# The third chunk of a graph is seeded by one ScalarE copy over both PSUM banks instead of one copy per bank

## What is computed

```python
def _L0_gnn_ref(x, adj, W1, b1, W2, b2):
    mask = (adj > 0.0).astype(x.dtype)
    xj_proj = x @ W1a
    diff = x[:, :, None, :] - x[:, None, :, :]
    h = jax.nn.relu(xj_proj[:, :, None, :] + diff @ W1b + b1)
    hm = jnp.einsum('bjkh,bjk->bjh', h, mask)
    deg = jnp.sum(mask, axis=-1)
    return hm @ W2 + deg[..., None] * b2
# layer 0
h = jnp.maximum(_layernorm(x, axis=-1), 0.0)
x = x + _L0_gnn_ref(h, adj, W1, b1, W2, b2)
# layer 1
h = jnp.maximum(_layernorm(x, axis=-1), 0.0)
x = x + einsum('bnm,bmf,of->bno', adj, h, W)
```

## Time and profile before

| | |
|---|---|
| median of 3 runs | 849.71 us (849.04 to 850.85) |
| profiled execution | 851.92 us, its span 849.9 us |
| busy: TensorE / VectorE / ScalarE / GpSimd | 95% / 96% / 93% / 72% |
| mean granted TensorE clock | 0.983 of 2.4 GHz |
| seeds L561 | 1024, 506 ns on the mean |
| gathers L400 of the regular chunks | 4096 |
| consumes L804 | 1024 |

### The profile page before, as it was taken

How to read it: one execution, slowest core, us unless ns; L and a number is a source line. 1 busy time by engine, 2 the same in 40 slices (tenths; PEclk the granted TensorE clock), 3 DMA queues, 4 the chain that set the end, 5 groups by cost and what they waited for, 6 DMA issues and landing times.

```text
span 849.9 us, 26682 instructions
## 1 busy us (share of the span) xinstructions
PE 809.7 (95%) x8242; PEld 712.0 (84%) x8243; DVE 820.1 (96%) x2908; ACT 794.5 (93%) x2241; POOL 610.8 (72%) x1164
## 2 busy tenths in 40 slices
PE   3779999999999999999999999999999999999996
PEld 1447888988898889888988898888888988998884
DVE  6989999999999999999999999999999999999994
ACT  4768999999999999999999999999999999999993
POOL 0855777777787777777777777777777777777773
PEclk9779999999999999999999999999999999999998
DMA  9800000000000000000000000000000000000000
GB/s 336 324 1 2 2 14 20 21 15 20 21 20 9 21 21 18 17 21 21 20 9 21 20 21 15 21 20 20 8 20 21 20 14 21 21 20 9 27 1 23
DMA packets 26704, 27.54 MB, mean 32 GB/s; under 512 B 3520, under 2 KB 24512, under 8 KB 25536
## 3 DMA queue, kind: packets, MB, share of 16 engines
q1 hardware_dynamic: 25488, 25.37, 8.8%
q10 hardware_dynamic: 1072, 0.43, 0.2%
HBM read 21.59 MB, written 4.19 MB: 30 GB/s over the span
## 4 chain that ended last, share of the span: by engine, by line
PE 84%; DVE 6%; issue 3%; ACT 3%; POOL 2%; DMA 1%; SPq 0%; ACTq 0%; POOLq 0%; DVEq 0%
PE ring L400 45%; PE ring L428 8%; PE prep L457 4%; DVE acc L804 4%; PE post L494 3%; PE post L500 3%; PE post L487 3%; PE post L488 3%; PE prep L465 3%; PE prep L468 2%; PE prep L463 2%; PE post L492 2%; POOL rstd L969 1%; DMA x_all<-x_nbf_dram 1%; PE prep L459 1%
## 5 line engine op out<-in xcount | busy, mean ns | idle before, releaser
L804 DVE SCALAR_TENSOR_TENSOR acc<-ring,acc 128x384 f32<-128x384 f32 x896 | 491.7, 549 | 0.6
L561 ACT COPY ring<-P 128x384 f32<-128x384 f32 x1024 | 467.5, 506 | 23.4 <-DVE acc L804 10.4
L400 PE MATMUL ring<-PQ,onehot_space 128*128 128x192 f16 x4096 | 418.7, 247 | 5.5 <-ACT ring L561 2.4
L400 PEld LDWEIGHTS ring<-PQ,onehot_space 128*128 128x128 f16 x4096 | 328.7, 99 | 42.7 <-issue 13.5
L900 POOL TENSOR_SCALAR start<-P,spare 128x192 f32<-128x192 f32 x128 | 131.9, 1030 | 135.5 <-ACT P L611 135.0
L924 POOL TENSOR_TENSOR row_space<-row_space 128x192 f32<-128x192 f32 x256 | 153.3, 599 | 29.7 <-ACT row_space L599 14.0
L790 DVE TENSOR_SCALAR onehot_space<-mask_all 128x512 f16<-128x512 f16 x512 | 161.8, 318 | 0.0
L428 PE MATMUL ring<-PQ,owner 128*128 128x384 f16 (+1 forms) x512 | 94.0, 306 | 0.0
L400 PE MATMUL ring<-PQ,onehot_row 128*128 128x192 f16 x768 | 84.4, 246 | 2.0 <-DVE onehot_row L852 2.0
L599 ACT ACTIVATE row_space<-ring 128x576 f32<-128x576 f32 x128 | 83.1, 649 | 0.7 <-PE ring L400 0.7
L804 DVE SCALAR_TENSOR_TENSOR acc<-ring,start 128x384 f32<-128x384 f32 x128 | 71.2, 556 | 6.8 <-PE ring L400 2.5
(11 more groups left out here) (138 smaller groups left out, 1422.0 us busy)
## 6 DMA issues: line engine op xcount, KB each, us to landing
onehot_space<-adj_kbj_dram SPq DMA_DIRECT2D x8, 1024.0 KB, 17.6
adj_again<-adj_kbj_dram SPq DMA_DIRECT2D x128, 64.0 KB, 2.0
x_all<-x_nbf_dram SPq DMA_DIRECT2D x8, 512.0 KB, 18.4
out_dram<-x_all SPq DMA_DIRECT2D x32, 128.0 KB, 1.9
consts<-consts_dram SPq DMA_DIRECT2D x1, 192.0 KB, 2.5
scratch<-w1a_dram ACTq DMA_DIRECT2D x2, 48.0 KB, 4.4
scratch<-w1b_dram ACTq DMA_DIRECT2D x2, 48.0 KB, 6.9
scratch<-b_dram ACTq DMA_DIRECT2D x1, 96.0 KB, 10.2
```

What stands on the lines that cost most here:

```text
L400: last = nc.tensor.matmul(to, hot(s), parts[:, part, H:2 * H], start=False, stop=(part == 1), skip_group_check=True)
L561: return nc.scalar.copy(slots[to][:, bank_], src.unsqueeze(1).broadcast_to([N, PER_BANK, H]))
L804: return nc.vector.scalar_tensor_tensor(sums, slots[to][:, bank_], 0.0, start[:, :, :] if first else sums, ALU.max, ALU.subtract if first ...
```

## The change

The third chunk of each graph (i = 2, listed in WHOLE) gets one copy of 768 elements over both banks, `seed_both`, in place of two copies of 384. It raises `seeded` once, so a graph now raises it seven times instead of eight; SEEDS holds the running count ahead of each chunk. TensorE waits, for both banks of that chunk, for the count that the one copy raises. The other chunks keep a copy and a count per bank. What the copies write is unchanged.

```diff
+SEEDS = (0, 2, 4, 5, 7)
+WHOLE = (2,)
...
                             for bank_ in range(BANKS):
-                                pe.wait_ge(seeded, (b * REGULAR + i) * BANKS + bank_ + 1)
+                                pe.wait_ge(seeded, b * SEEDS[-1] + (SEEDS[i + 1] if i in WHOLE else SEEDS[i] + bank_ + 1))
                                 dst = [(s, slot(place(u, i), s)) for s in range(PER_BANK * bank_, PER_BANK * (bank_ + 1))]
                                 gather(dst, parts, hot).then_inc(gathered, 1)
...
+            def seed_both(to, src):
+
+                return nc.scalar.copy(slots[to], src.unsqueeze(1).unsqueeze(1).broadcast_to([N, BANKS, PER_BANK, H]))
+
...
-                        for bank_, consumed in enumerate((half_summed, summed)):
-                            if i in (0, 1) and exists(b - 1):
-                                act.wait_ge(consumed, b * REGULAR - 1 + i)
+                        if i in WHOLE:
                             if i == 3:
-                                act.wait_ge(consumed, b * REGULAR + 1)
-                            seed(place(u, i), P[:, u % 2, :], bank_).then_inc(seeded, 1)
+                                act.wait_ge(summed, b * REGULAR + 1)
+                            seed_both(place(u, i), P[:, u % 2, :]).then_inc(seeded, 1)
+                        else:
+                            for bank_, consumed in enumerate((half_summed, summed)):
+                                if i in (0, 1) and exists(b - 1):
+                                    act.wait_ge(consumed, b * REGULAR - 1 + i)
+                                if i == 3:
+                                    act.wait_ge(consumed, b * REGULAR + 1)
+                                seed(place(u, i), P[:, u % 2, :], bank_).then_inc(seeded, 1)
```

## The result

The changed kernel takes 858.54 us against 850.83 for the kernel before, medians of 17 runs each taken side by side: ratio 1.0092, interval 1.0072 to 1.0112, 7.7 us slower. Forecast were 5.7 us more, in a range of 848 to 866.

The account below looks back on a forecast made before the run. The prediction took a slackless ring through TensorE, VectorE and ScalarE, once per pair of graphs, as the bound. 63 pairs x 0.09 us = 5.7 us on the median 849.71 gave 855.4 us, range 848 to 866.

Parts of the forecast that it names:

- the bounds: Limits on the whole copy's length around the forecast 0.82 us: 0.79 us below, 0.92 us above.
- S-to-L478: Even graph, third chunk's first seed start to TensorE's L478: about 2.15 us before, 2.19 to 2.29 forecast.
- 63 x 0.09: 63 graph pairs, each longer by the even graph's middle delay of 0.09 us: 5.7 us slower.
- the ring: Even-graph seeds, TensorE, VectorE and back, 11.95 us a pair; delay added to S-to-L478 lengthens the pair fully.
- second ring: Runs over odd-graph seeds and the even graph's first consume; delayed 0 to 0.09 us, beside the first, not added.
- where the 0.10 us goes: ScalarE's saving per graph brings P and later work earlier, ends waiting for VectorE's consume, and shortens nothing on the ring.
- Rival A: L790 slips behind GpSimd's row sums L924 in even graphs, up to 0.33 us each; 862 to 876 us; chance 0.12.
- Rival B: Odd-graph L790 moves further behind L924 and loses 0.18 us; 846.4 or 850.5 us; chance 0.18.
- Rival C: ScalarE bounds the kernel, so 0.10 us less a graph gives 12.8 us less, 836.9 us; chance 0.05.
- Rival D: The even-graph delay falls into idle time, so no effect, 849.7 us; chance 0.07.

Follow-up runs that it names:

- e1_wait: Kernel before with two copies kept, but the third chunk's gathers for both banks wait for the second copy; 858.91 against 851.38 us.
- e7_whole3: Changed kernel with the whole copy given to the fourth chunk instead of the third; 878.06 us against 850.41 for the kernel before.
- e2_filler: Changed kernel plus a one-column ScalarE copy behind the fourth chunk's seeds, filling the saved 0.1 us; 854.44 us against 851.38 for the kernel before.
- f2_light_whole: Changed kernel with GpSimd's row sums and second fp16 part of P cut to one column each; 859.11 us against 850.41 for the kernel before.
- f3_light_whole_hold: f2_light_whole with GpSimd's start sums held back to a later VectorE consume; 846.16 us against 852.27 for the kernel before.
- the three kernels with the hold: Start sums held back on the kernel before, the changed kernel and e5_order_whole; 896.39, 895.41 and 894.98 us against 852.27.
- e3_short: Kernel before with ScalarE's PQ copy cut from 384 to 272 columns, so P comes earlier; 846.72 against 851.38 us.
- f1_light: Kernel before with GpSimd's row sums and second fp16 part of P cut to one column each; 841.69 against 850.41 us.
- e4_order: Kernel before with ScalarE's code_row and ownerT copies moved behind the fourth chunk's seeds; 850.62 against 851.38 us.
- e5_order_whole: Changed kernel with code_row and ownerT moved behind the fourth chunk's seeds; 849.05 us against 850.41 for the kernel before.
- g1_hold: Kernel before with only GpSimd's start sums held back to a later VectorE consume, nothing left out; 896.39 against 852.27 us.

## Why the prediction was right, and where it was not

**The copy.** Forecast 0.82 us and a spacing of 0.72 to 0.73; measured 827 ns and 0.73. The interpolation from a copy's own slope was right and the bounds weren't needed. The Trainium skill (ScalarE: Activation LUTs, What ACT_TABLE_LOAD costs) gives 186 ns + 0.833 ns an element, an estimate of 0.83 us for this copy; the 827 ns agree.

**S-to-L478.** Forecast 2.19 to 2.29, measured 2.21 in the graph shown and 2.27 on the mean of all even graphs, 0.09 more than before, the forecast's middle; 2.38 in e1_wait and 2.37 in e7_whole3 in the graphs shown (2.37 and 2.44 on the mean), each as their expectations had it. This step holds.

**From the delay to the time.** Forecast 63 x 0.09 = 5.7 us (2.5 to 8.8). With that delay of 0.09 and P unmoved, e2_filler costs 3.0 us; e1_wait, with one of 0.20 (2.374 against 2.176 on the mean), costs 7.5. That is 33 and 38 us for each microsecond of delay in the even graph, not 63. What is wrong is "the ring has no slack": it was read from one pair, in which VectorE waits 0.10 us for the odd graph's first gathers. Over the whole trace before, VectorE waits ahead of 66 of 128 first consumes (43 of 64 in odd graphs, 23 in even ones), so a delay passes on only in part, and L790, which gets shorter with the delay, gives some of it back. In f2_light_whole, f3_light_whole_hold and the three kernels with the hold nearly all of VectorE's idle time ahead of first consumes stands in even graphs (15.5 of 16.9 us in f3_light_whole_hold): that is the prediction's second ring, over the odd graph's seeds, which it did not add.

**The step that failed** is "where the 0.10 us goes ... it shortens nothing". It shortened nothing on the ring, and ScalarE's gain did end in a wait for VectorE (10.4 to 25.4 us). But the 0.1 us costs the other 4.7 of the 7.7 us: with ScalarE put back by a filler they are gone. That it does so by moving GpSimd's operations against VectorE's is read from the traces (4.4 us more of VectorE's busy time, more long row one-hots), not shown by a run of its own: f2_light_whole and f3_light_whole_hold show such a cost for another meeting, with the start sums. So the delay was priced at 5.7 us where it costs 3.0, and the gain at nothing where it costs 4.7. That the total came near the forecast is in part luck, two errors of opposite sign.

**Rival A**, a new collision, was right in kind and wrong in place. I had L790 at 400.80 behind the row sums; the operations that got longer are the row one-hots behind the second fp16 part of P, and `from_first`. I looked at one pair of operations and not at all that wait for P.

**Rival B**, the collision at L790 eases: it did, from 318 to 299 ns on the mean, (318 - 299) x 512 = 9.7 us of busy time, nearly the 9 us that it was priced at. But e1_wait has 297 ns and e2_filler 304, so it comes with the later gathers, with or without an earlier P. In e2_filler VectorE is 4.7 us less busy than before; in the changed kernel other operations take longer and the 4.7 are gone but for 0.3.

**Rival C** (ScalarE is the bound, -12.8 us) fell: less ScalarE work with the wait gave +7.7, and 4.7 us were gained only where the cut stood ahead of P without a wait (e3_short). **Rival D** fell too: the delay of 0.09 us is there, and even alone it costs 3.0 us.

**What stays open.** Why the earlier P gains 4.7 us in the kernel before and loses as much with the later gathers. The traces show which operations get longer in the one case, but no run moved GpSimd by known steps with all else fixed, and f1_light warns that an operation's mean length does not tell its price. Nor does anything here say why the runs of the changed kernel spread over 10 us. By the 33 to 38 us for a microsecond, e7_whole3's 0.27 us of delay would cost some 10 us, an estimate; what makes up the rest of its 27.7 is not found either. Also open is why e4_order's ring, shorter by some 0.3 us, returned 0.8 us in all; the longer L790 (326 ns there) is the place found, not a proof. No version was found that is clearly better than the kernel before and computes P and Q with the same two parts; e5_order_whole, at 0.9986, comes nearest.

## What to carry to other kernels

Joining two operations frees the engine a little, but delays whoever waited for the first half; compare the new end with the old start of the consumer, and follow that delay round until it meets an engine that waits, and count over the whole trace how often it does. Do the same for everything that comes earlier by it: where two engines get in each other's way, an operation that starts 0.1 us sooner can cost more than the delay does. Test the two halves apart, with a filler of the saved length for one of them.

## What the runs showed of the hardware

A VectorE one-hot of 0.28 us took 0.42, 0.56 and 0.61 us where a GpSimd operation on SBUF had begun 0.15, 0.04 and 0.13 us ahead of it (the start sums, x_all, the row sums), and `from_first`, 0.25 us, took 0.63. A row one-hot of 0.18 took up to 0.54 in the changed kernel:

```profile
L863 DVE TENSOR_SCALAR onehot_row<-code_row x384: 174/182/546, 64.2 to 842.5; 128x128 f16<-128x128 f16 x192
```

Where VectorE began first, as at 404.27 against 404.66, its operations kept their length: in the traces of all runs none of the one-hots that began while GpSimd was idle, with its next operation starting during them, took more than 0.30 us (row one-hots 0.20). Such meetings need not average out: in g1_hold and f2_light_whole they fall in nearly every pair at the same place, and g1_hold takes 5% longer.

A ScalarE copy into PSUM over two banks costs no more than its elements: 827 ns for 768 against 506 for 384, 0.84 ns for each further element, where 192 to 384 elements in one bank take 0.81.
